# Router logits with the weights stationary: one attention and mixture-of-experts block on one core

## What is computed

```python
h = jnp.take(L0_tok_weight, x, axis=0)                      # (32, 128, 256)
h = h + attention(_layernorm(h), q_proj, k_proj, v_proj, o_proj)   # 16 heads, causal
xf = _layernorm(h).reshape(N, D)
logits = xf @ wg                                            # (4096, 256) @ (256, 8)
scores = jax.nn.softmax(logits, axis=-1)
top1 = jnp.argmax(scores, axis=-1)
combine_w = jnp.take_along_axis(scores, top1[:, None], axis=1)[:, 0]
rank = (place of the token among those of its expert)
slot = jnp.where(rank < capacity, top1 * capacity + rank, trash)
h = jax.nn.gelu(eb @ W1 + b1, approximate=False)            # eb: the rows of each expert
y = h @ W2 + b2
out = h_before + gathered(y, slot) * combine_w
```

## Time and profile before

| | us |
|---|---|
| median of 3 runs | 623.44 (623.02 to 623.56) |
| the profiled execution | 626.09 |
| its span, first to last instruction | 624.4 |
| attention phase, until the first instructions of the experts | 357.0 |
| TensorE busy | 576.3 (92%) |
| VectorE busy | 419.6 (67%) |
| ScalarE busy | 338.8 (54%) |
| GpSimd busy | 258.3 (41%) |

### The profile page before, as it was taken

The page is one execution under the profiler, slowest core; times in us unless marked ns, Lnnn a source line. Parts: engine busy times, 40 slices in busy tenths (PEclk is TensorE's granted clock), DMA queues, the critical chain, the costliest instruction groups (busy, mean ns, idle before and its releaser), DMA issues. The chain is left out here.

```text
span 624.4 us, 14332 instructions
## 1 busy us (share of the span) xinstructions
PE 576.3 (92%) x5311; PEld 498.5 (80%) x5371; DVE 419.6 (67%) x1073; ACT 338.8 (54%) x708; POOL 258.3 (41%) x316
## 2 busy tenths in 40 slices
PE   6778899989999999999898799999999999999993
PEld 3466677877877877787665369999999999999993
DVE  6255678988898888888766266565656575757531
ACT  2233555555555556555462168585858585858550
POOL 5445777765556655565563200404030403040303
PEclk9897999999999999999999999999999999999997
DMA  4678777546786644556111132151515151511101
GB/s 124 202 245 282 239 224 227 160 147 225 230 252 212 194 149 135 157 161 222 35 36 69 45 115 98 35 180 39 179 35 180 33 180 35 177 36 45 33 2 32
DMA packets 42581, 84.39 MB, mean 135 GB/s; under 512 B 6822, under 2 KB 32987, under 8 KB 38864
## 3 DMA queue, kind: packets, MB, share of 16 engines
q1 hardware_dynamic: 35600, 70.66, 35.6%
q0 software_dynamic: 6144, 12.67, 6.4%
q10 hardware_dynamic: 768, 0.13, 0.1%
HBM read 52.64 MB, written 31.74 MB: 135 GB/s over the span
## 5 line engine op out<-in xcount | busy, mean ns | idle before, releaser
L1009 POOL DMA_INDIRECT out_dram<-ys,xs x48 | 50.1, 1045 | 218.6 <-DVE ys L1206 209.1
L400 POOL TENSOR_SCALAR_AFFINE_SELECT pt<-pt 128x512 f32<-128x512 f32 x128 | 81.9, 640 | 86.0 <-ACT pt L442 84.5
L442 ACT ACTIVATE pt<-C 128x512 f32<-128x512 f32 x128 | 76.5, 598 | 72.1 <-PE C L616 68.1
L1219 DVE TENSOR_TENSOR hl<-gl,hh 128x324 fp32r<-128x324 f32 x128 | 63.3, 495 | 38.7 <-ACT hh L1049 34.1
L796 DVE TENSOR_REDUCE mx<-S 128x4 f32<-128x512 f32 x128 | 86.7, 681 | 4.0 <-PE S L602 2.2
L1049 ACT ACTIVATE hh<-gl 128x324 fp32r<-128x324 f32 x128 | 61.7, 491 | 0.0
L602 PE MATMUL S<-ks,qs 96*128 96x128 bf16 x512 | 50.2, 220 | 8.6 <-issue 6.6
L715 PE MATMUL PV<-pt,va 128*32 128x128 f32 x1024 | 54.1, 284 | 1.6 <-ACT os L449 0.8
L602 PEld LDWEIGHTS S<-ks,qs 96*128 96x128 bf16 x512 | 40.1, 98 | 15.7 <-issue 0.6
L616 PE MATMUL C<-qs,ks 97*128 97x128 bf16 x512 | 50.3, 220 | 1.0 <-DMA qs<-nm 1.0
L1206 DVE SCALAR_TENSOR_TENSOR ys<-C,xs 108x256 f32<-108x256 f32 x48 | 21.8, 481 | 40.1 <-PE C L1099 36.9
(11 more groups left out here) (157 smaller groups left out, 1706.8 us busy)
## 6 DMA issues: line engine op xcount, KB each, us to landing
w_raw<-in_L_ffn_W_dram SPq DMA_DIRECT2D x16, 1024.0 KB, 8.7
qs<-q_parts SPq DMA_DIRECT2D x48, 256.0 KB
ks<-k_parts SPq DMA_DIRECT2D x48, 256.0 KB
q_parts<-qp SPq DMA_DIRECT2D x16, 384.0 KB, 2.4
k_parts<-kp SPq DMA_DIRECT2D x16, 384.0 KB
rows_of_slots<-w_raw SPq DMA_DIRECT2D x6, 877.5 KB
xs<-rows_of_slots SPq DMA_DIRECT2D x8, 658.1 KB
out_dram<-h SPq DMA_DIRECT2D x16, 256.0 KB
```

The source lines that it names most:

```text
L400: pool.affine_select(out=buf[:, :, :], in_=buf[:, :, :], compare_op=ALU.is_ge, fill=0.0, base=0, pattern=[[0, 4], [1, S]], channel_multipl ...
L442: act.activation(pt[u % 4][:, :, :], bC[u % 2][:, :].rearrange("p (j t) -> p j t", j=4), ACT.Exp, scale=SCALE).then_inc(a_exp, 1)
L1009: pool.indirect_dma_start(out=outf, out_offset=bass.IndirectOffsetOnAxis(ap=xs[e.slot][:, j, D + 3:D + 4].bitcast(U32), axis=0), in_=ys[j] ...
L1219: dve.tensor_tensor(hl[:, f, cols], gl[u % 4][:, :], hh[:, f, cols].bitcast(F32), ALU.subtract).then_inc(v_hl, 1)
```

## The change

The logits' matmuls swap their sides. The weights `wgs` are now padded with zeros to 32 columns and are stationary; the 128 tokens of a sequence stream. The two sequences go to two column tiles of 32 columns (partitions 0 to 31 and 32 to 63 of `bM2`). The result has the experts on partitions, so ScalarE copies it to `lgs` (64x128) and TensorE turns it back in one transpose in slot 7; `route` waits for that transpose. VectorE clears `wgs` ahead of its load. The filler matmuls of step 0 become 18, and stand ahead of the wait on `v_xn` instead of behind it.

```diff
-        wgs = sb("wgs", [P, KC, E], F32)
+        wgs = sb("wgs", [P, KC, 32], F32)
+        lgs = sb("lgs", [GB * 32, S], F32)
...
-            sp.dma_start(wgs[:, :, :], wg.rearrange("(k p) e -> p k e", p=P)).then_inc(d_c, 16)
+            sp.wait_ge(v_wgs, 1)
+            sp.dma_start(wgs[:, :, 0:E], wg.rearrange("(k p) e -> p k e", p=P)).then_inc(d_c, 16)
...
                 scores(6)
+                if g5:
+                    wait(act, pe_lg, g5.times(1, 1))
+                    act.activation(lgs[:, :], bM2[0:GB * 32, 0:S], ACT.Copy).then_inc(a_lg, 1)
                 scores(7)
...
                     if g and s == 7:
+                        if g.off == 1:
+                            idle_work(bPV, 18)
                         wait(pe, v_xn, g.times(1, 1))
-                        if g.off == 1:
-                            idle_work(bPV, 14)
...
                     if g and s == 6:
                         wait(pe, a_x2t, g.times(1, 1))
-                        for b in range(GB):
-                            for k in range(KC):
-                                last = pe.matmul(bM2[:, b * E:(b + 1) * E], x2t[:, k, b * S:(b + 1) * S],
-                                                 wgs[:, k, :], start=(k == 0), stop=(k == KC - 1))
+                        for k in range(KC):
+                            for b in range(GB):
+                                last = pe.matmul(bM2[32 * b:32 * b + 32, 0:S], wgs[:, k, :],
+                                                 x2t[:, k, b * S:(b + 1) * S], start=(k == 0), stop=(k == KC - 1))
                         last.then_inc(pe_lg, 1)
+                    if g and s == 7:
+                        wait(pe, a_lg, g.times(1, 1))
+                        pe.transpose(bM2[:, 0:GB * 32], lgs[:, :], identf[0:GB * 32, 0:GB * 32]).then_inc(pe_lgT, 1)
...
         def _(dve):
+            dve.memset(wgs[:, :, :], 0.0).then_inc(v_wgs, 1)
...
-                lg = bM2[:, 0:GB * E].rearrange("p (b e) -> p b e", b=GB)
-                wait(dve, pe_lg, g.times(1, 1))
+                lg = bM2[:, 0:GB * 32].rearrange("p (b e) -> p b e", b=GB)[:, :, 0:E]
+                wait(dve, pe_lgT, g.times(1, 1))
```

More of the change, by code:

```diff
@@ L233, in attention_phase @@
         v_xf, pe_id, v_idt, pe_w, a_wh, v_wl = (sem(n) for n in ("v_xf", "pe_id", "v_idt", "pe_w", "a_wh", "v_wl"))
-        pe_bias, v_bias, v_blank = sem("pe_bias"), sem("v_bias"), sem("v_blank")
+        pe_bias, v_bias, v_blank, v_wgs = sem("pe_bias"), sem("v_bias"), sem("v_blank"), sem("v_wgs")
+        pe_lgT, a_lg = sem("pe_lgT"), sem("a_lg")
         pe_T, pe_Q, pe_K, pe_V, pe_S, pe_mT, pe_C, pe_PV, pe_OT, pe_oT, pe_O, pe_x2T, pe_lg, pe_rk = (
```

## The result

The changed kernel takes 623.17 us (median of 20 runs, 621.19 to 624.73), the kernel before on the same chip 624.71 (20 runs, 623.02 to 627.23). The ratio is 0.9973, with an interval from 0.9960 to 0.9986: faster by 1.5 us at the medians, where 4.0 was forecast. The change was measured twice more: 0.9943 (0.9923 to 0.9963) and 0.9995 (0.9977 to 1.0013). The three intervals do not all overlap, so the gain is best given as 0 to 0.6%, around 0.3%. The kernel before itself had medians of 624.71, 626.22, 627.62 and 625.02 in the four comparisons, so only kernels timed side by side are set against each other. The profiled execution of the change has a span of 621.3 us, 3.1 less than that of before. Half of this belongs to the execution of before that was profiled, which took 626.09, 1.4 above the median of the 20 runs.

A forecast was written before the change was run, and what follows sets the result against it. TensorE's own list was taken to bound the full steps, the DMA queue the first steps. Start -3.0, full steps -1.5, last steps +0.5 made -4.0 us, from 623.44 to 619.4; range 617.0 to 622.6.

The forecast's parts named there:

- The transpose back: Extra transpose of the logits in slot 7 of a full step: +0.06 us on TensorE, up to 0.15 in the range.
- The logits: Logits block on TensorE in slot 6 of a full step: 0.66 us instead of 0.86, 0.20 less.
- the term of -1.5: Sum over the 11 full steps, steps 5 to 15, at -0.14 us each; bounds -0.6 and +4.3.
- What was hidden: ScalarE's 0.25 us copy falls into its wait for C; VectorE's `lmax` does not wait for the transpose: no cost.
- the rival of tiles that do not run side by side: Logits' two column tiles do not overlap: +1.8 us at worst, -1.8 with half the overlap, 621.6 to 625.2; chance 0.09.
- The fillers: Step 0: 18 fillers inside the wait for `v_xn`, transposes 4.5 us earlier, of which -3.0 us arrives (1.5 to 4.5).
- the landing of `ks` of group 0: First steps: stacks issued by 25.6 are there between 30.5 and 31, so group 0's first scores gain 3.3 us.
- the rival of the DMA queue: First steps: the DMA queue takes the start's gain back, leaving -1.0 us in all, 622.4; chance 0.12.
- The last steps: Router on the path for the last two groups: first logit matmul to `lmax` 1.38 us, 0.28 more; +0.5 us in all.

The follow-up runs named there:

- full_rows: The changed kernel with `lgs` over 128 partitions, upper 64 zeros, all turned by the transpose back: 622.50 us, 0.9943 of the kernel before.
- fillers_blanks: The kernel before with 18 fillers ahead of the wait on `v_xn` and the blank rows' DMAs in steps 3 to 5: 625.88 us, 0.9962.
- cover_ks: The changed kernel with 20 fillers instead of 8 in slot 4 of step 1: 623.90 us, 0.9989 of the kernel before.
- before_blanks: The kernel before with the six blank-row DMAs in steps 3 to 5, two each, instead of one each in steps 0 to 5: 626.35 us, 0.9986.
- after_third: The changed kernel itself, measured a third time: 623.75 us, 0.9995 of the kernel before.
- Fillers_only: The kernel before with 18 fillers ahead of the wait on `v_xn` instead of 14 behind it, nothing else: 627.10 us, 1.0016.
- router_no_fillers: The changed kernel without its 18 fillers in step 0: 624.07 us, 0.9988 of the kernel before.
- router_only: The changed kernel with step 0's 14 fillers back behind the wait on `v_xn`: 626.28 us, 0.9993 of the kernel before.
- after_again: The changed kernel itself, measured a second time: 624.41 us, 0.9943 of the kernel before.
- tiles_by_pv: full_rows with the logits' block moved behind the transposes of `os`, directly ahead of PV: 620.48 us, 0.9905 of the kernel before.
- tiles_no_fillers: tiles_by_pv without any filler in step 0: 620.11 us, 0.9939 of the kernel before.

## Why the forecast was wrong

**The transpose back failed.** I took 0.06 us and kept 0.15 for the range; it costs 0.20. I chose the small value by the transpose of the maxima, which has 128 rows and 32 columns and pays nothing. The new one has 64 rows of 128, and pays on its way in; full_rows, which has all 128 rows and streams 128 columns instead of 64, wins 0.10 a step. The Trainium skill (TensorEngine Tiling (Array Packing)) lists 64 rows by 128 columns as a configuration of its own (Available Configurations) and says that a change of mode drains the engine (Key Properties). The trace agrees that there is a price, 0.10. I had set a near row above the rule, though the row showed another dimension. The other 0.05 was that half the streamed columns do not take half the time: less the 0.09 of PV's entry, the 0.20 from the transpose to PV leave 0.11, as for one of the full width.

**The logits were right.** 0.21 measured, 0.20 forecast, from PV's row and two more passes a tile. The tiles ran side by side. So a full step wins 0.01 instead of 0.14, and the term of -1.5 is near 0. What was hidden stayed hidden: the transpose is ready at 251.36 and `lmax` starts at 251.68. (In the rival of tiles that do not run side by side, half the overlap makes +0.08 a step, not 0.06.)

**The fillers failed, as the rival said.** I took -3.0 for the start. The transposes did come 4.0 us earlier, but the first scores only 0.8. The step that failed is the landing of `ks` of group 0. I put it at 30.5 to 31, by taking the 2.4 us of the blank block off the end of the full queue at 33, which makes some 5 us behind the last issue. It takes 6.6 in the change (issued by 26.90, there at 33.52), 6.4 to 7.6 in the ten other profiles in which TensorE waits for it, and 6.5 in fillers_blanks, where no blank block stands behind it; so that block could not be taken off. The issue itself is 1.3 later than the 25.6 of before: `q_parts` are issued 0.7 later in this execution, and travel 0.7 longer beside running fillers (3.12 against 2.45).

What was left was gone by group 1. `qs` of group 1 is issued when it was before, the queue being full until 37, and the idle time of 3.0 us is followed by a stretch at half clock, at a place where there was none. Which of the two took it is not settled: fillers_blanks has the queue free and cover_ks the clock up, and neither is told from its partner on the same chip (before_blanks, after_third); both at once were not tried. Fillers_only (1.0016) and router_no_fillers (0.9988 beside 0.9995) put the fillers' worth within about 1 us of nothing. I had given the rival of the DMA queue 0.12; the queue row, empty from 33 to 35, was read as room that an earlier issue would fill, but the earlier issue only found it full. That the rival's -1.0 lies near the measured -1.5 is luck: it counted -1.5 for the full steps, which did not come.

**The last steps were half right.** From group 13's `lmax` to group 15's after_third loses 0.46 us, forecast 0.5; the last `lmax` follows the first logit matmul by 1.31, forecast 1.38, before 1.10. In the three emptying steps before that it gains 0.27 to 0.36 each, which I had not counted; that the shorter block of logits is what gains there is argued, not shown.

**One gain was not foreseen.** Between groups 5 and 8 the change wins 1.40 us in each of its first and third profile. The four other kernels with the old router win 0.60 to 0.75 there too, so about half belongs to the one execution of before. Most of it is a single wait that before has in step 7, on TensorE:

```profile
129.42 0.36 PE L570 MATMUL M<-xth,wh 128*128 128x256 f32 x1 [1.26 <-DVE xtl L803]
```

It starts on ScalarE, whose releaser the profile does not name:

```profile
127.46 0.60 ACT L510 ACTIVATE va<-M 128x512 f32<-128x512 f32 x1 [2.39 <-remote]
```

TensorE waits there for 0.6 to 0.8 us in the four other kernels with the old router, 0.41 in router_only, after_again and full_rows, 0.37 and 0.38 in tiles_by_pv and tiles_no_fillers, and not at all in the change, after_third, cover_ks and router_no_fillers. So it is shorter with the new router; that after_again, the change's own program, has 0.41 shows that it varies from one execution to the next. What holds ScalarE back in that step was not tried and stays open.

## What to carry to other kernels

Count what a short matmul does to the array's shape on both sides, rows as well as columns, and put work of one shape together: a padded transpose of the full 128 rows was faster than one of 64, and two blocks of column tiles side by side were faster than two entries. Where a stretch is bound by DMAs, follow the first transfer to its landing before counting a gain ahead of it on an engine; TensorE's earlier start became a wait, with a stretch at 1.2 GHz behind it. Before "issue" waits are read as slack, compare the counts of matmuls between stretches of equal work, since missing records look the same.

## What the hardware showed that I had not expected

- Entering a 64-row transpose from 128-row ones cost 0.10 us (0.53 against 0.43 from the transposes of `xn`), while a 32-column transpose with all rows cost nothing.
- Matmuls of different column tiles overlap across blocks: PV's first tile started 0.10 us before the last logits, and both blocks took 0.79 us instead of 0.92.
- From the issue of `q_parts` to that of `qs`, which waits for its landing, it took 3.0 to 4.0 us in eight profiles with fillers on TensorE at that moment, and 2.45 to 2.56 in six without them. Why is open.
- Less time at 1.2 GHz in the first steps did not show in the time: until 60 us cover_ks has 6.8 us of it and after_third 10.2, and their medians are 0.15 us apart.
- `ks` landed 6.4 to 7.6 us behind the end of its issue in eleven profiles, and 6.5 in the one of them that has no block of blank rows behind it in the queue.
